# Masking block attention by two half-height exponentials instead of by extra matmuls

## The reference

```python
H, bs = 8, 64; dk = D // H; nb = S // bs            # 8 heads of 128, 32 blocks of 64 tokens
q = (src @ Wq + bq).reshape(B, nb, bs, H, dk)       # k and v alike
scores = einsum('bnqhd,bnkhd->bhnqk', q, k) * dk ** (-0.5)
probs  = softmax(scores, axis=-1)                   # only keys of the query's own block
out    = einsum('bhnqk,bnkhd->bnqhd', probs, v).reshape(B, S, D)
x = layernorm(src + out @ Wo + bo)
x = layernorm(x + einsum('bsi,oi->bso', x, sign(weight)))
```

## Time and profile before

| what | value |
|---|---|
| time, median of 2 runs | 447.76 us (447.33 to 448.19) |
| the profiled execution, its own time | 450.9 us |
| its slowest core, the one of the profile | core 2, span 449.3 us |
| spans of all cores | 442.0 to 449.3 us |
| PE busy | 342.2 us, 76% of the span |
| VectorE (DVE), ScalarE (ACT) busy | 168.3 and 137.7 us |
| packets' share of 16 DMA engines' time | 31.8% on GpSimd's queue, 20.6% on SP's |

### The profile page before, as it was taken

The page is one execution under the profiler, slowest core; times in us unless marked ns, Lnnn a source line. Parts: engine busy times, 40 slices in busy tenths (PEclk is TensorE's granted clock), DMA queues, the critical chain, the costliest instruction groups (busy, mean ns, idle before and its releaser), DMA issues.

```text
span 449.3 us, 6072 instructions; the slowest of 8 cores (442.0 to 449.3 us)
## 1 busy us (share of the span) xinstructions
PE 342.2 (76%) x2128; PEld 198.6 (44%) x2128; DVE 168.3 (37%) x400; ACT 137.7 (31%) x269; POOL 27.4 (6%) x44
## 2 busy tenths in 40 slices
PE   0003918689519999999999999989999999996450
PEld 0002803328304477438545844764386448442110
DVE  5000004131105642744366156327542752464323
ACT  0000602234701425325340723252335317241100
POOL 3001012100000010010001000000100000000000
PEclk9999976998869999999999999999999999998665
DMA  7999969992471482165246413841572431133002
GB/s 96 175 181 180 208 103 127 146 191 95 92 142 23 72 230 53 35 157 139 48 93 143 140 25 70 236 48 23 127 180 47 76 113 36 24 37 117 6 18 94
DMA packets 71168, 46.55 MB, mean 104 GB/s; under 512 B 59847, under 2 KB 59873, under 8 KB 71138
## 3 DMA queue, kind: packets, MB, share of 16 engines
q0 software_dynamic: 11952, 31.47, 31.8%
q1 hardware_dynamic: 59186, 14.70, 20.6%
HBM read 37.77 MB, written 8.39 MB: 103 GB/s over the span
## 4 chain that ended last, share of the span: by engine, by line
PE 58%; DMA 26%; ACT 4%; issue 4%; SPq 3%; DVE 3%; POOL 1%; DVEq 0%; ACTq 0%; POOLq 0%
PE pb L378 19%; PE pb L614 14%; PE pb L525 11%; PE pb L406 8%; DMA wv_sb<-wv 6%; DMA wq_sb<-wq 4%; DMA masku<-mask_scratch 3%; DMA sws_sb<-wf 3%; DMA ln1fm<-ln1bf 3%; SPq L336 2%; PE psc L453 2%; PE pb L530 2%; DMA x_bf<-x 2%; DMA probsT<-probsn 2%; PE psc L448 2%
## 5 line engine op out<-in xcount | busy, mean ns | idle before, releaser
L378 PE MATMUL pb<-x_fm,wq_sb 128*128 128x256 bf16 x512 | 60.2, 281 | 43.3 <-DMA x_fm<-x_bf 43.3
L614 PE MATMUL pb<-swt_sb,ln1fm 128*128 128x512 bf16 x256 | 64.8, 411 | 24.9 <-DMA ln1fm<-ln1bf 14.3
L378 PEld LDWEIGHTS pb<-x_fm,wq_sb 128*128 128x128 bf16 x512 | 50.9, 101 | 52.0 <-issue 44.9
L525 PE MATMUL pb<-wo_sb,ao_sb 128*128 128x512 bf16 x256 | 62.0, 386 | 0.5
L378 PE MATMUL pb<-x_fm,wk_sb 128*128 128x256 bf16 x512 | 59.1, 276 | 3.7 <-ACT k_fm L391 3.7
L406 PE MATMUL pb<-wv_sb,x_fm 128*128 128x512 bf16 x256 | 57.9, 385 | 0.0
L378 PEld LDWEIGHTS pb<-x_fm,wk_sb 128*128 128x128 bf16 x512 | 50.2, 99 | 11.1 <-issue 3.9
L391 ACT ACTIVATE q_fm<-pb,bcol 128x256 bf16<-128x256 f32 x64 | 26.7, 470 | 86.6 <-PE pb L378 86.6
L614 PEld LDWEIGHTS pb<-swt_sb,ln1fm 128*128 128x128 bf16 x256 | 25.8, 104 | 59.8 <-issue 37.3
L624 DVE SCALAR_TENSOR_TENSOR r<-pb,ln 128x512 f32<-128x512 f32 x32 | 21.5, 688 | 79.1 <-PE pb L614 79.1
L469 DVE TENSOR_REDUCE ssum<-probsn 128x8 f32<-128x1024 bf16 x16 | 19.5, 1220 | 76.7 <-ACT probsn L462 76.7
(11 more groups left out here) (84 smaller groups left out, 204.9 us busy)
## 6 DMA issues: line engine op xcount, KB each, us to landing
x_tm<-x POOLq DMA_DIRECT2D x8, 1024.0 KB, 6.6
y<-outb POOLq DMA_DIRECT2D x7, 1024.0 KB, 5.0
x_bf<-x POOLq DMA_DIRECT2D x8, 512.0 KB, 8.5
wq_sb<-wq POOLq DMA_DIRECT2D x1, 2048.0 KB, 20.0
wk_sb<-wk POOLq DMA_DIRECT2D x1, 2048.0 KB, 32.6
wv_sb<-wv POOLq DMA_DIRECT2D x1, 2048.0 KB, 25.0
wo_sb<-wo POOLq DMA_DIRECT2D x1, 2048.0 KB, 26.6
sws_sb<-wf POOLq DMA_DIRECT2D x8, 256.0 KB, 6.9
```

What stands on the lines that cost most here:

```text
L378: last = e.matmul(bank[:, mi * GTOK:(mi + 1) * GTOK], wt[:, kk * D + m * 128: kk * D + (m + 1) * 128], x_fm[:, slot * 2048 + kk * GTOK: sl ...
L525: e.matmul(bank[:, 0:512], ao[:, s * 1024 + kk * 128: s * 1024 + (kk + 1) * 128], wo[:, kk * D + hf * 512: kk * D + (hf + 1) * 512], start ...
L614: last = e.matmul(bank[:, 0:512], ln1fm[:, kk * GTOK + s * 128: kk * GTOK + (s + 1) * 128], swt[:, kk * D + hf * 512: kk * D + (hf + 1) * ...
```

## The change

The mask is gone: its tensors, memsets, three DMAs and matmuls. Every score matmul is now a whole accumulation of its own (`start=True, stop=True`), and the off-diagonal blocks of `psc` hold real scores that nobody reads. `emit_exp_s` becomes two instructions. Each handles the 64 queries of one block (64 partitions) and, for the 8 heads, the 64 keys of the same block, and writes only those into `probsn`. The other blocks of `probsn` keep the zeros of the memset at the start, since the division multiplies zero. The sum, the division, the transposes and the products with V work on 128 keys as before.

```diff
-        def mkmrow(e):
-            e.memset(mrow[0:1, 0:64], 1.0)
...
-        P.stage("dve", mkmrow, writes=[Bmrow])
-        Bmscr = Buf()
-        P.stage("sp", lambda e: e.dma_start(mscr_h, mrow[0:1, 0:1280]),
-                reads=[Bmrow], writes=[Bmscr])
-        P.stage("gp", lambda e: e.dma_start(
-            masku[:, :], bass.AP(mscr_h.tensor, 0, [[128, 2], [1, 128]])),
-            reads=[Bmscr], writes=[Bmask])
-        P.stage("gp", lambda e: e.dma_start(
-            maskv[:, :],
-            bass.AP(mscr_h.tensor, 256, [[512, 2], [1, 512]])),
-            reads=[Bmscr], writes=[Bmask])
...
         def emit_scores_s(g, s):
             def scfn(e, s=s):
                 last = None
-                for half in range(2):
-                    for hh in range(4):
-                        h = half * 4 + hh
-                        e.matmul(
-                            psc[:, h * 128:(h + 1) * 128],
-                            q_fm[:, h * GTOK + s * 128: h * GTOK + (s + 1) * 128],
-                            k_fm[:, h * GTOK + s * 128: h * GTOK + (s + 1) * 128],
-                            start=(hh == 0), stop=False)
+                for h in range(H):
                     last = e.matmul(
-                        psc[:, half * 512:(half + 1) * 512],
-                        masku[:, :], maskv[:, :],
-                        start=False, stop=True)
+                        psc[:, h * 128:(h + 1) * 128],
+                        q_fm[:, h * GTOK + s * 128: h * GTOK + (s + 1) * 128],
+                        k_fm[:, h * GTOK + s * 128: h * GTOK + (s + 1) * 128],
+                        start=True, stop=True)
                 return last
-            P.stage("pe", scfn, reads=[Bqfm, Bkfm, Bmask], writes=[Bpsc])
+            P.stage("pe", scfn, reads=[Bqfm, Bkfm], writes=[Bpsc])
 
         def emit_exp_s(g, s):
-            def expfn(e, s=s):
-                return e.activation(
-                    probsn[:, s * 1024:(s + 1) * 1024], psc[:, :],
-                    AF.Exp, scale=SCALE)
-            P.stage("act", expfn, reads=[Bpsc], writes=[Bprobsn[s]])
+            for half in range(2):
+                def expfn(e, s=s, half=half):
+                    q0 = 64 * half
+                    return e.activation(
+                        probsn[q0:q0 + 64, s * 1024:(s + 1) * 1024].rearrange(
+                            "p (h k) -> p h k", h=H)[:, :, q0:q0 + 64],
+                        psc[q0:q0 + 64, :].rearrange(
+                            "p (h k) -> p h k", h=H)[:, :, q0:q0 + 64],
+                        AF.Exp, scale=SCALE)
+                P.stage("act", expfn, reads=[Bpsc], writes=[Bprobsn[s]])
```

More of the change, by code:

```diff
@@ L131, in build_program @@
     y_h = nc.dram_tensor("y", [S, D], F32, kind="ExternalOutput").ap()
-    mscr_h = nc.dram_tensor("mask_scratch", [1, 1280], BF16, kind="Internal").ap()
     dbg_h = {}
@@ L160, in build_program @@
         onesb = sb("ones_bf", [1, 256], BF16)
-        masku = sb("masku", [2, 128], BF16)
-        maskv = sb("maskv", [2, 512], BF16)
         x_tm = sb("x_tm", [128, 4096], F32)
@@ L212, in build_program @@
         Beps = Buf()
-        Bmask = Buf()
         Bxtm = [Buf(), Buf()]
@@ L288, in build_program @@
         P.stage("dve", lambda e: e.memset(onesb[:, :], 1.0), writes=[Bones])
-        Bmrow = Buf()
-        mrow = ln1bf
-        def mkmrow(e):
-            e.memset(mrow[0:1, 0:64], 1.0)
[L295 to L305, removed]
-        P.stage("dve", mkmrow, writes=[Bmrow])
-        Bmscr = Buf()
-        P.stage("sp", lambda e: e.dma_start(mscr_h, mrow[0:1, 0:1280]),
-                reads=[Bmrow], writes=[Bmscr])
-        P.stage("gp", lambda e: e.dma_start(
-            masku[:, :], bass.AP(mscr_h.tensor, 0, [[128, 2], [1, 128]])),
-            reads=[Bmscr], writes=[Bmask])
-        P.stage("gp", lambda e: e.dma_start(
-            maskv[:, :],
-            bass.AP(mscr_h.tensor, 256, [[512, 2], [1, 512]])),
-            reads=[Bmscr], writes=[Bmask])
         P.stage("dve", lambda e: e.memset(epsc[:, :], EPS), writes=[Beps])
@@ L595, in emit_ln1 @@
                     scale=istd1[:, s:s + 1]),
-                    reads=[Br[s], Bis1, Bng1], writes=[Bln1bf[s], Bmrow]
-                    if g == 0 else [Bln1bf[s]])
+                    reads=[Br[s], Bis1, Bng1], writes=[Bln1bf[s]])
                 def lfmfn(e, s=s):
```

## The result

| | before | after |
|---|---|---|
| median time | 446.92 us (30 runs) | 444.46 us (31 runs) |
| ratio, with its 95% interval | | 0.9933 (0.991 to 0.9956) |
| spans of the 8 cores in the profiled execution, mean | 444.2 us | 439.5 us |
| PE busy in the profiled execution | 342.2 us | 324.2 us |

The change gains 0.7%, 3.0 us by the ratio, where I had forecast 3.3%: 433.1 us in a range of 428 to 440. By the border of 2% that the prediction names, this is no change. In some executions some neighbouring cores show a granted clock of 0.80 to 0.89 in place of 0.94 and end 15 to 50 us later (in 11 of 14 executions of e2, e7 and e8, 5 of 6 of e12 and none of 13 of e9, e10 and e11; why isn't shown), so where an experiment had mostly such executions I give the times of the others and read the cores that kept their clock.

The account below looks back on a forecast made before the run. DMA engines were taken to bound the kernel until Q of group 1, PE from group 2 on. Masks -8.96, start -6, exponentials +0.3 sum to -14.7 us: from the median 447.76 to 433.1, range 428 to 440.

Parts of the forecast that it names:

- the border of 2%: Whole kernel: changes of about 2%, 9 us, can be told from none, so faster means below 438.8 us.
- Part 1, the masks: PE, groups 1 to 7: 28 mask matmuls at 0.32 us leave the path, saving 8.96 us; remaining scores keep their time.
- The estimate from the Trainium skill: Mask matmuls on PE: an isolated-gap formula gave 216 ns each, 6.0 us for 28; the trace's 0.32 us was preferred.
- Part 2, the start: Before Q of group 1: without the masku wait, Q starts at about 95 instead of 101.1, gaining 6 us, range 0 to 12.
- the hole closed: DMA engines at 62 to 66 us: earlier sws_sb pieces fill the roughly 4 us in which they ran dry, gaining 4 us.
- its 1 MB takes 4 us of the engines: Transposes before Q of group 1: the early x_tm load of group 2 could cut the 6 us gain to 2 or nothing.
- My own sign of being wrong: Start: the prediction is wrong if Q of group 1 starts after 99 or before 91 us.
- at about 90: GpSimd's queue: x_tm of group 2 issued at about 90 us instead of 100.66, as group 0's attention ends up to 11 earlier.
- Part 3, the exponentials: ScalarE, each subtile: two half exponentials take 1.10 us, 0.08 more than one; 0.3 us charged in all, range 0 to 6.5.
- rival C: Each group: a half exponential costs like a whole one, adding 4 to 6.5 us, 437 to 440; sign: waits for probsT; chance 0.09.
- The rigid shift: From Q of group 1 to group 2: signs, layer norm and ten transposes simply move with the start of Q.
- A: Start: gives only 0 to 2 us, as early x_tm slows transposes or the ring paces pieces; 437 to 439.5; chance 0.20.

Follow-up runs that it names:

- e2: Changed kernel with the loads x_tm of groups 1 and 2 and x_bf of group 2 held until x_fm of group 1 landed; median 449.29 us, undisturbed cores 423.1 to 430.2.
- e7: Changed kernel with x_bf of group 2 issued ahead and x_tm of groups 1 and 2 held until x_fm of group 1 landed; 430.45 us, median of all executions 449.32.
- e8: The kernel of e2 run again, all three loads held back; 430.0 and 432.95 us, median of all executions 449.19.
- e12: The kernel of e1 with a two-row matmul of zeros put back after each four scores; 444.34 us, median of all six executions 468.96.
- e9: The kernel of e2 plus 28 unread filler matmuls ahead of Q of group 1; 430.66 us, ratio 0.9634.
- e10: The kernel of e9 with the second half of the signs and eight transposes of sws_sb moved ahead of Q of group 1; 422.34 us, ratio 0.9434.
- e11: The kernel of e1, no fillers, with the second half of the signs and eight transposes of sws_sb moved ahead of Q of group 1; 420.62 us, ratio 0.9413.
- e1: Changed kernel with x_tm of group 2 held until x_fm of group 1 landed; 436.31 us, ratio to before 0.9737.
- experiment 2: Kernel before, mask matmuls and single exponential kept, with only the DMAs of masku and maskv moved to SP's queue; 455.73 us, ratio 1.0219.
- experiment 6: Changed kernel with one full 128 x 1024 exponential in place of the two, off-diagonal blocks left unmasked; 444.81 us, ratio 0.9906.
- Experiment 9: The two kernels e10 and e11, with signs and transposes of sws_sb moved ahead of Q of group 1; 422.34 and 420.62 us.

## Why the prediction was wrong, point by point

**Part 1, the masks** was right in kind and too small. I took 0.32 us for each and let the scores "keep their time", by the rows of the attention output, whose eight matmuls take 0.66. They do not keep it: eight scores take 0.45 us without masks between them and 0.22 + 0.33 with. The period fell by 1.70 us and not by 1.28, so groups 1 to 7 gave 7 x 1.70 = 11.9 us in place of 8.96; the stages show 11.8. (VectorE also lost 19 memsets for the mask rows, not 15; they lie at 6.6 us and after and are no piece of the chain.) The estimate from the Trainium skill that I had set beside it (216 ns, 6.0 us) is off by a factor of two here.

**Part 2, the start** is where the prediction failed. The steps up to it held: `masku` out of the chain, the hole closed (share 1.10 and 1.16 in 62 to 66), `x_bf` issued at 77.96 on core 2, first scores at 57.8 to 60.5. The first transposing DMA comes 4.6 us earlier in the mean of the cores, of the 6 that I had. The step that failed is "its 1 MB takes 4 us of the engines [...] the gain of this part is 6 - 4 = 2 us, or nothing", and the choice to keep 6 "because the load arrives when the transposes are mostly issued". It arrives 0.5 to 3.3 us after the first one, and costs them 8 us in the mean (16.9 against 8.9), 14 on core 0. I had seen the row that said so, a transposing DMA of 12.43 us in the busy start against 3.85 later, three times as long, and used it as a word of caution instead of as the price. Then PE, idle for 16 to 22 us, begins Q at 1.2 GHz (granted clock 0.50), and Q takes 2 us more. My own sign of being wrong, Q of group 1 after 99 us, came on all eight cores. The measured time fell by 3.0 us; with 11.8 from the loop and 1.6 lost at the end, which no term of my sum had, the start cost about 7 us instead of giving 6. Experiments 1 and 2 show it from both sides.

When `x_tm` of group 2 would be issued I had worked out from PE's earlier end ("at about 90"). It came at 85.2 to 87.0 on six of the cores and at 91.1 and 91.7 on cores 0 and 6. On five cores (0, 3, 5, 6, 7) the residual sum still decides: the load is issued 0.70 us after its last instruction. On the other three (1, 2, 4) that sum is done so early that another condition decides, the ring: the third predecessor of the load is `x_bf` of group 1, the very load that the transposes wait for. There it goes 0.5 us behind the first transposing DMA, and the order of the queue makes the two start together. The cores with the longest transposes are 0 and 6 (22.6 and 18.8 us), where the load came 2.1 and 3.3 us behind the first one, so a load that comes while transposes are being issued was no better than one that comes with them.

The sentence on the rule of the Trainium skill that would have warned me: DMA: Bandwidth & Descriptors, Queues, rings and completion order, says that each DMA engine serves the queue rows that have work in turn, packet by packet. Equal turns of equal packets would at most double the 4.7 us that the transposes need alone, 9.4 us, an estimate with that page's rule. The trace agrees in direction, and goes beyond that: 13.4 to 22.6 us.

But the packets aren't equal. The page of before has (queue: packets, MB, share of 16 engines; q0 is GpSimd's, q1 SP's):

```profile
q0 software_dynamic: 11952, 31.47, 31.8%
q1 hardware_dynamic: 59186, 14.70, 20.6%
```

The 59,186 packets of SP's queue moved 14.70 MB, 248 bytes each, in 20.6% of the time of 16 engines; the 11,952 of GpSimd's queue moved 31.47 MB, 2.6 KB each, in 31.8%. That is 0.025 us of an engine for a packet of the one and 0.19 for one of the other, 7.6 times as much. If turns went by these packets and both queues always had some, the 4.7 us could become 4.7 x 8.6 = 40 us, an estimate from these rows. What was measured lies between the two. These rows stood there before the change and give a bound far above the 4 us that I took from the load's bytes. That packet size is the reason was not tested.

**Part 3, the exponentials** was right: 0.592 us each and 1.21 for a pair (1.10 forecast), and no loss of time by experiment 6. The chain does pass through `probsT` after the change, which I had named as the sign of rival C. It is not one: PE was idle about 0.6 us ahead of the second attention output before, and is idle 0.59 now, in group 3 of core 2, by its timeline:

```profile
228.88 0.66 PE L471 MATMUL pb<-probsT,v_tm 128*128 128x128 bf16 x8 [0.59 <-DMA probsT<-probsn]
```

And the period is the same with one exponential. Only in group 2 the transpose of `probsn` lands late (4.81 us), and that period is 40.56 us on core 2; this is a remainder of 0.4 to 1.3 us, once.

**The rigid shift.** I took the stretch from Q of group 1 to Q of group 2 as shifting rigidly. It did (59.6 us before, 59.4 after, with 1.7 less for the masks and 1.5 to 2 more for the lower clock). Experiment 9 shows that it didn't have to stay as it was.

**Rivals.** A named the right mechanism, with the chance 0.20, and bounded it at no loss (437 to 439.5, measured 444.46). Nothing in the trace gave that bound: the lower end came from the bytes of the load and not from what happens to the transfers beside it.

**What stays open.** How the engines divide their time between a load and the transposes beside it is measured and not explained; no run varies the size of the packets alone. Why the end of the kernel takes 1.6 us more once the mask DMAs leave GpSimd's queue is not shown either.

## What to carry to other kernels

When a change lets an early stage finish sooner, list every load that this stage's end releases, and look at which latency-critical transfer is in flight at that time; price the meeting by the slowest such transfer that the trace already shows, and look at the packet sizes of the two queues, rather than go by the load's bytes over the bandwidth. Making work end earlier that isn't on the path can cost more than it gives (experiment 2), and one added wait on a load that isn't urgent (here, `x_tm` of group 2) can be worth more than the whole change. A fixed block of work behind the bound (here the signs and ten transposes) should be asked first whether it needs to stand there.

## What the runs showed of the hardware

- The two transposing DMAs of `x_fm` on SP's queue suffer far more from loads beside them than the bytes say: 4.7 us to Q alone (e8), 8.2 to 8.9 with 1.5 MB of loads that started 2 to 10 us earlier (e1, before), 13 to 23 when a further 1 MB load starts 0.5 to 3.3 us behind them (after). On core 0 of after the DMA share is 1.10 to 1.29 meanwhile, and only 105 to 110 GB/s are moved.
- A matmul with two rows and 512 columns between 128-column ones costs 0.425 us of PE's time, though its row says 0.32: what follows it is slower by 0.1.
- On every core of every profiled execution on which PE had idled 4.2 to 22.4 us just ahead of Q of group 1, Q began at 1.2 GHz (granted clock 0.50), and its 64 matmuls of 256 columns took 8.4 to 10.1 us in place of 7.15. Behind pauses of 0 to 1.6 us it ran at a granted clock of 1.00 throughout. Behind pauses of 1.7 to 2.3 us the clock fell in the course of Q on four cores (8.8 us, two of them of before).
- An exponential of 64 partitions x 512 elements, in runs of 64, takes 0.592 us and a pair 1.21, against 1.02 for the 128 x 1024 one: the strides and the half height cost no time that experiment 6 can tell. The pair is 0.19 us longer than the one.
- The end of the kernel, from the issue of the last `y` store, takes 4.8 to 4.9 us on all cores where GpSimd's queue has the two mask DMAs, and 6.4 to 6.9 on all cores where it doesn't.
